# Attention 1 of a ViT block: the scaling of k moved from VectorE to GpSimd

## The reference

```python
qkv = x @ w_qkv.T
q, k, v = (t.reshape(b, n, h, dh).transpose(0, 2, 1, 3) for t in split(qkv))
q = q * rsqrt(norm(q, axis=1) + EPS)      # the norm runs over the 12 heads
k = k * rsqrt(norm(k, axis=1) + EPS)
dots = einsum('bhid,bhjd->bhij', q, k)
scores = softmax(dots / scale[:, None, None])
out = einsum('bhij,bhjd->bhid', scores, v)
return out.reshape(b, n, h * dh) @ w_out.T + b_out
```

## Time and profile before

| | us |
|---|---|
| median of three runs | 4624.5 |
| lowest, highest | 4619.6, 4639.1 |
| profiled execution | 4633.1 |
| its span, first to last instruction | 4631.2 |
| PE busy / DVE / ACT / POOL in the span | 3955.3 / 2938.5 / 2372.0 / 533.5 |
| mean granted TensorE clock, share of full speed | 0.917 |

### The profile page before, as it was taken

How to read it: one execution, slowest core, us unless ns; L and a number is a source line. 1 busy time by engine, 2 the same in 40 slices (tenths; PEclk the granted TensorE clock), 3 DMA queues, 4 the chain that set the end, 5 groups by cost and what they waited for, 6 DMA issues and landing times.

```text
span 4631.2 us, 87675 instructions
## 1 busy us (share of the span) xinstructions
PE 3955.3 (85%) x32408; PEld 3447.0 (74%) x32408; DVE 2938.5 (63%) x7313; ACT 2372.0 (51%) x3969; POOL 533.5 (12%) x861
## 2 busy tenths in 40 slices
PE   3888888888888888888888888888898888888887
PEld 3777777777777777777777777777777777777776
DVE  3666666666666666666666666666666666667664
ACT  1555554554555555545545545555555455455553
POOL 2110110101101101101011011011011010110110
PEclk7999999998999899989999999999999999989997
DMA  3111111111111111111111111111111111111110
GB/s 86 31 38 39 32 42 41 30 40 45 30 39 38 38 39 38 38 39 30 40 45 30 39 46 30 39 38 38 39 32 44 39 30 39 46 31 39 40 25 19
DMA packets 87586, 176.71 MB, mean 38 GB/s; under 512 B 15802, under 2 KB 28733, under 8 KB 87134
## 3 DMA queue, kind: packets, MB, share of 16 engines
q1 hardware_dynamic: 87230, 170.98, 14.5%
HBM read 44.45 MB, written 9.68 MB: 12 GB/s over the span
## 4 chain that ended last, share of the span: by engine, by line
PE 56%; DVE 15%; SPq 8%; DMA 8%; issue 7%; ACT 4%; POOL 1%; DVEq 0%; ACTq 0%; POOLq 0%
PE psum L570 11%; SPq L371 8%; PE psum L577 7%; PE psum L520 6%; PE psum L503 5%; DVE mx L905 5%; PE psum L559 5%; PE psum L561 4%; DMA kb<-low 4%; DVE low L900 4%; DMA qb<-high 4%; PE psum L605 3%; PE psum L635 3%; PE psum L628 2%; PE psum L544 2%
## 5 line engine op out<-in xcount | busy, mean ns | idle before, releaser
L905 DVE TENSOR_REDUCE mx<-psum 99x4 f32<-99x788 f32 x768 | 711.0, 973 | 216.9 <-PE psum L544 214.3
L717 ACT ACTIVATE ebuf<-psum 99x788 f32<-99x788 f32 x768 | 605.4, 823 | 214.3 <-PE psum L561 209.6
L559 PE MATMUL psum<-qa,ka 128*99 128x197 f16 x3072 | 592.4, 256 | 30.3 <-DVE qb L918 29.5
L544 PE MATMUL psum<-ka,qa 128*99 128x197 f16 x3072 | 407.9, 285 | 229.0 <-DMA kb<-low 107.6
L561 PE MATMUL psum<-qb,kb 128*99 128x197 f16 x3072 | 583.7, 253 | 0.0
L544 PEld LDWEIGHTS psum<-ka,qa 128*99 128x99 f16 x3072 | 342.9, 148 | 280.8 <-issue 184.3
L570 PE MATMUL psum<-ebuf,vx 98*128 98x197 f32 (+1 forms) x3072 | 551.2, 331 | 0.0
L570 PEld LDWEIGHTS psum<-ebuf,vx 98*128 98x128 f32 (+1 forms) x3072 | 508.7, 190 | 0.0
L683 ACT ACTIVATE qk_sq<-psum 128x788 f32<-128x788 f32 x192 | 159.0, 828 | 626.6 <-PE psum L520 626.6
L446 POOL TENSOR_TENSOR veps<-mv,eps_ln 99x2 f32<-99x2 f32 x256 | 50.1, 196 | 3573.4 <-DVE mv L815 2923.2
L559 PEld LDWEIGHTS psum<-qa,ka 128*99 128x99 f16 x3072 | 394.5, 128 | 88.8 <-DVE mx L905 43.4
(11 more groups left out here) (148 smaller groups left out, 6380.1 us busy)
## 6 DMA issues: line engine op xcount, KB each, us to landing
ka<-high SPq DMA_DIRECT2D x256, 148.5 KB, 2.6
xb<-x_t SPq DMA_DIRECT2D x64, 591.0 KB, 3.9
qa<-high SPq DMA_DIRECT2D x128, 148.5 KB, 2.5
qa<-low SPq DMA_DIRECT2D x128, 148.5 KB, 2.7
qb<-high SPq DMA_DIRECT2D x128, 148.5 KB, 2.8
kb<-low SPq DMA_DIRECT2D x128, 148.5 KB, 2.7
out<-h SPq DMA_DIRECT2D x128, 73.5 KB
vx<-w_qk SPq DMA_DIRECT2D x1, 1152.0 KB
```

Of the source, the lines that this page charges most:

```text
L544: mm = nc.tensor.matmul(ps(p, slice(0, TR), slice(NT * t, NT * t + NT), e), qa[s][:, h if kind == "SM" else h // 4, tile_cols(t)], ka[s][: ...
L559: nc.tensor.matmul(o, ka[s][:, h, tile_cols(t)], qa[s][:, g, 0:NT], start=True, stop=False)
L717: nc.scalar.activation(ebuf[n % EBUFS][:].rearrange("p e a t -> p e (a t)"), psum[0:TR, b:b + 2, 0:2 * NT], ACT.Exp).then_inc(done, 1)
L905: nc.vector.tensor_reduce(mx[s][:, :, 2 * i:2 * i + 2].rearrange("p a e -> p e a"), psum[0:TR, b:b + 2, 0:2 * NT].rearrange("p e (a t) -> ...
```

## The change

The multiply of N.2 goes from VectorE's program to GpSimd's. It reads and writes the same tensors and waits for the same semaphore `rr_ready`, on GpSimd now. It raises a new semaphore, `k_scaled`; `qkn_ready` no longer counts N.2. ScalarE's cast in N.3 waits for `k_scaled` in place of `qkn_ready`, and the cast in N.1 for N.0 as before. N.0, N.1 and N.3 and the order of the steps stay as they are.

```diff
-        qkn_ready = signal("qkn_ready", ("N",))
+        qkn_ready = signal("qkn_ready", ("N",), lambda p: p[2] != 2)
+        k_scaled = signal("k_scaled", ("N",), lambda p: p[2] == 2)
...
+                    elif p[0] == "N" and p[2] == 2:
+
+                        wait(pool, now, rr_ready, ("PS", s, 0))
+                        nc.gpsimd.tensor_tensor(qk[s][:, 6:12, :], qk[s][:, 6:12, :],
+                                                nrm[s][:, NT:2 * NT].unsqueeze(1).broadcast_to([128, 6, NT]),
+                                                ALU.mult).then_inc(k_scaled[1], 1)
...
-                        wait(act, now, qkn_ready, ("N", s, i - 1))
+                        wait(act, now, *((qkn_ready, ("N", s, 0)) if i == 1 else (k_scaled, ("N", s, 2))))
...
-                    elif kind == "N":
+                    elif kind == "N" and i != 2:
...
-                        elif i == 2:
-
-                            a = nc.vector.tensor_tensor(qk[s][:, 6:12, :], qk[s][:, 6:12, :],
-                                                        nrm[s][:, NT:2 * NT].unsqueeze(1).broadcast_to([128, 6, NT]),
-                                                        ALU.mult)
```

## The result

| | before | after |
|---|---|---|
| median of four runs, us | 4631.8 | 4802.2 |
| lowest, highest | 4619.6, 4643.0 | 4786.4, 4814.1 |
| profiled execution / its span | 4633.1 / 4631.2 | 4803.3 / 4801.5 |
| mean granted TensorE clock | 0.917 | 0.909 |

The ratio is 1.037, with a 95% interval of 1.032 to 1.041: the change makes the kernel slower by 170 us, 2.66 us for each of the 64 images. The median of before has moved by 7 us from the one of the prediction, since one more run counts in it.

A forecast was written before the change was run, and what follows sets the result against it. The prediction took the spread chain, with TensorE waiting for k's copies before SM.0, as the bound. A full hold, 64 images x 2.8 us = 179 us, gave 4804 us, 3.9% slower; range 4617 to 4865 us.

The forecast's parts named there:

- the spread chain: Per image N.0, N.1, DMA, N.3, DMA, SM.0: normalising, casting and copying q and k, which TensorE waits for, 1.7 us per image.
- N.2's removal is worth 0: On VectorE: the 1.37 us multiply has 1.2 us to spare before q's copies land, so removing it gains 0.
- GpSimd takes 2.88 us: The moved multiply of 1182 elements on GpSimd: 0.06 us fixed plus 2.38 ns per element, priced from its two-input fp32 operations.
- A full hold: At N.0, VectorE's second operation waits until GpSimd's multiply is done, so N.0 ends 2.88 us late; chance 0.52.
- 2.8 us at N.1's `low`: N.1's `low` on VectorE starts 2.8 us later: 2.88 us of hold less 0.1 us given back at QK2.0.
- Nothing behind it takes the delay up or adds to it: From N.1 to SM.0: the casts and copies pass on the 2.8 us, 179 us over 64 images.
- The range's upper edge: Total time: 4865 us, from a hold of 2.8 us per image with 1 us of clock.
- The clock as an upper edge only: TensorE's granted clock during longer waits: up to 1 us per image, 64 us, as upper edge and nothing in the forecast.
- `kb<-low` still last at SM.0: Before SM.0, the landing of k's copies still ends TensorE's wait, as in all 64 images before.
- TensorE waits longer before SM2.0: At SM2.0, TensorE waits for VectorE's `kb`, done at 2064.78 behind the held N.0; a longer wait was the sign.
- Held late (rival 1): GpSimd starts only after N.0 and holds N.1's `low` by 1.5 us: 96 us, 4721 us; late or partial hold, chance 0.20.
- The rule against the row: At N.0, the skill's mutual exclusion in SBUF gives 179 us; trace row L1019, unhindered beside a GpSimd operation, gives 0.

## Why the prediction was right

The forecast was 4804 us and 1.039 of before; measured are 4802 and 1.037 (1.032 to 1.041). The mechanism, a hold of N.0 that the spread chain passes on, is shown; that the two times agree so closely is luck, as its terms show. Point by point:

- *N.2's removal is worth 0.* Held. The kernel with the multiply behind N.1 has VectorE rid of N.2 without any hold, and its ratio is 1.000; the kernel with N.2 kept and the hold added loses as much as the change within the noise. SM2.0's row maxima start 0.33 us earlier in the first of the two (median) and not 0.5, and that buys nothing.
- *GpSimd takes 2.88 us.* 2.48 measured. The slope of 2.38 ns per element came from additions of two full tensors; the multiply's second input is one row repeated six times. Between 394 columns (0.95 us) and 1182 the multiply has 1.94 ns per column and 0.18 us fixed. Whether the operation or the repeated row makes it cheaper is open. This is the mis-sized term.
- *A full hold.* Held, and GpSimd's length sets it: 2.32 us for 2.48, 0.79 for 0.95. The place was wrong: the first operation of N.0 is held, not the second. So the hold starts at once and not 0.4 us later, and N.0 is longer by 0.16 us less than GpSimd is busy.
- *2.8 us at N.1's `low`.* 2.12 measured. Of the difference, 0.56 is the mis-sized hold (2.88 against 2.32) and 0.1 is that N.0's delay gives back 0.2 us at QK2.0 and not 0.1.
- *Nothing behind it takes the delay up or adds to it.* The first half held. The second failed: the copies of q landed late in 30 images, 0.55 us per image in the mean. So 2.12 + 0.55 = 2.67 us came close to my 2.8 by two errors of opposite sign; the total is nearer to the forecast than its terms are. The range's upper edge was also added up wrongly: 4624.5 + 64 x 3.8 is 4868 and not 4865, far from the measured time.
- *The clock as an upper edge only.* 0.909 against 0.917; it was not needed for the sum, since behind SM.0 an image takes as long as before.
- *`kb<-low` still last at SM.0.* In 49 images of 64. That TensorE waits longer before SM2.0 held.
- *Held late (rival 1).* Its price, 96 us, was too low: put there by hand, the multiply held the fp16 copy of QK2.0, which the rival didn't count, and cost 185 us.
- *The rule against the row.* The rule of the Trainium skill ("SBUF — State Buffer", section "Who interferes with whom") decided rightly that there is a hold, and L1019 is no proof of none: that GpSimd operation reads two columns, and a two-column add holds almost nothing in the experiments either. "For the whole instruction" doesn't fit those. Nor does the order: by the rule the one that starts second is blocked, and here the VectorE operation has the earlier start by 0.04 us in all 64 images and is the one held.

## What to carry to other kernels

Before work is moved to GpSimd, look at what VectorE does in the same microseconds: an operation with two SBUF inputs, or an fp16 copy like the one here, can stand still for nearly as long as GpSimd reads, and shows as a long operation, not as idle time. Move the GpSimd work beside operations that were not held here (one input in PSUM, or the masked multiplies), at a place with slack, by a wait on another signal; cutting it in six didn't help. And an offload pays only if the step is near the bound: here it was worth nothing until k's halves had buffers of their own and N.3 its earlier place, and then about 2%.

## What the runs showed of the hardware

In the late images one packet of the queue that the profile calls "instruction" falls among q's copies. The DMA view of after, an odd image, from N.1's `low` to shortly before the cast of N.3, in two stretches: until 2209.3, and from then on. Then the same of before, where the packet comes when the copies are all but done. Columns: packets, MB, share of 16 engines.

```profile
q1 hardware_dynamic: 413, 0.80, 73.3%
...
q1 hardware_dynamic: 67, 0.11, 19.6%
q8 instruction: 1, 0.02, 3.1%
```

```profile
q1 hardware_dynamic: 469, 0.91, 75.9%
...
q8 instruction: 1, 0.02, 9.4%
q1 hardware_dynamic: 11, 0.00, 0.8%
```

In before the packet starts 5.14 us or more behind the end of `low` in 30 of the odd images, here with 11 packets of the copies left, and none is late. In after it starts 4.5 to 4.7 us behind it in 28 of these images, here with 67 left, and in the other two at 5.0 and 5.2; all 30 are late, by 0.7 to 1.6 us. In the kernel with a third of the multiply 13 of the 30 have the packet at 4.5 to 5.0 us, and these 13 are late, the 17 with the packet at 5.1 us or later are not. So a delay in the program moved copies under a packet that the kernel's text doesn't issue. That the packet causes the lateness is argued from this and not shown. The packet itself wasn't moved, and some images don't fit: the late one with it at 5.2 us, and in the kernel with the multiply in six pieces four more with it at 5.2 to 5.4 us, late by 1.5 to 1.7.
